# Moving the values' 5x5 depthwise convolution into the attention stage of a four-layer network kernel

## The reference, cut to what matters

```python
x = x + dwconv(x, pos_w, pos_b)                  # 3x3
xn = layer_norm(x, ln1_g, ln1_b)
q, k, v = xn @ q_w + q_b, (xn @ k_w + k_b) * HD ** -0.5, xn @ v_w + v_b
lepe = dwconv(v, lepe_w, lepe_b)                 # 5x5, each channel by itself, 'SAME' edges
q, k = theta_shift(q, sin, cos), theta_shift(k, sin, cos)
o = softmax(q @ k.T + mask) @ v                  # per image and head, 1024 x 1024 scores
x = x + (o + lepe) @ out_w + out_b
```

## Time and profile before

| | |
|---|---|
| three executions | 3669.94, 3670.02, 3678.01 us, median 3670.02 |
| the profiled execution | 3670.32 us |
| its span in the profile | 3668.7 us |
| outside the span | 1.6 us |
| values made token by token | to 219.95 us |
| `depthwise` of the values | 220.2 to 297.3 us |
| attention | 297.9 to 1046.7 us |
| GRU and the later layers | from about 1300 us |
| busy over the whole span | PE 86%, DVE 70%, ACT 50%, POOL 16% |

### The profile page before, as it was taken

The page is one execution under the profiler, slowest core; times in us unless marked ns, Lnnn a source line. Parts: engine busy times, 40 slices in busy tenths (PEclk is TensorE's granted clock), DMA queues, the critical chain, the costliest instruction groups (busy, mean ns, idle before and its releaser), DMA issues. The chain is left out here.

```text
span 3668.7 us, 136690 instructions
## 1 busy us (share of the span) xinstructions
PE 3141.9 (86%) x50394; PEld 2339.4 (64%) x50394; DVE 2582.0 (70%) x12076; ACT 1821.7 (50%) x5594; POOL 583.8 (16%) x2420
## 2 busy tenths in 40 slices
PE   5378999999958947999999999999999998577787
PEld 1134666566622315888988888889888887254454
DVE  4567999999974635777777777777777778466562
ACT  2215999999933025444544444444444445133342
POOL 0001111111100001222222222222222222111110
PEclk9678999999978966555555555555555555678888
DMA  1312333333330000000000000000000000000000
GB/s 32 108 47 95 108 107 107 107 107 107 108 91 1 10 7 2 5 5 5 5 5 5 5 5 5 5 5 5 5 5 5 5 5 4 11 1 1 0 5 13
DMA packets 54608, 116.12 MB, mean 32 GB/s; under 512 B 12313, under 2 KB 19801, under 8 KB 53692
## 3 DMA queue, kind: packets, MB, share of 16 engines
q1 hardware_dynamic: 37104, 53.42, 5.3%
q0 software_dynamic: 13824, 50.34, 3.9%
q10 hardware_dynamic: 2956, 3.15, 0.4%
HBM read 84.06 MB, written 22.81 MB: 29 GB/s over the span
## 5 line engine op out<-in xcount | busy, mean ns | idle before, releaser
L504 PE MATMUL g_zr<-g_hp,g_wp 97*128 97x4 f16 x24576 | 1082.6, 171 | 53.4 <-issue 49.0
L504 PEld LDWEIGHTS g_zr<-g_hp,g_wp 97*128 97x128 f16 x24576 | 956.4, 108 | 157.4 <-issue 51.3
L595 ACT ACTIVATE g_e<-g_tn 96x8 f32<-96x8 f32 x2048 | 437.0, 213 | 557.8 <-DVE g_tn L540 557.8
L480 PE MATMUL g_zr<-s_inner,g_wi 96*128 (+2 forms) x6240 | 585.1, 234 | 61.9 <-issue 39.7
L612 POOL COPY s_y<-g_hs 96x8 f32 x2048 | 401.0, 196 | 1374.9 <-DVE g_hs L555 1374.9
L553 DVE TENSOR_TENSOR_SCAN g_hp<-g_gates,g_e 96x16 f16<-96x16 f32 x2048 | 382.1, 187 | 316.7 <-ACT g_e L595 207.6
L592 ACT ACTIVATE g_gates<-g_zr 96x16 f32<-96x16 f32 x2048 | 399.5, 195 | 315.5 <-PE g_zr L504 315.4
L511 PE MATMUL g_n<-g_hp,g_wp 97*128 97x8 f16 x8192 | 520.1, 174 | 0.0
L844 DVE CUSTOM_DVE_ANT_0 a_negated<-a_scores,a_mask 128x1024 f32<-128x1024 f32 x384 | 468.0, 1219 | 59.1 <-PE a_scores L762 41.2
L870 ACT ACTIVATE a_probs<-a_negated,a_negmax 128x1024 f32<-128x1024 f32 x384 | 442.4, 1152 | 26.1 <-DVE a_negmax L844 16.3
L540 DVE TENSOR_TENSOR_SCAN g_tn<-g_gates,g_n 96x24 f32<-96x24 f32 x2048 | 387.8, 189 | 95.7 <-ACT g_gates L592 95.7
(11 more groups left out here) (324 smaller groups left out, 3058.5 us busy)
## 6 DMA issues: line engine op xcount, KB each, us to landing
a_mask<-in_L_mask POOLq DMA_DIRECT2D x96, 512.0 KB, 5.6
a_k<-k_rows SPq DMA_DIRECT2D x96, 144.0 KB
q_rows<-r_q_parts SPq DMA_DIRECT2D x12, 576.0 KB, 7.4
k_rows<-r_k_parts SPq DMA_DIRECT2D x12, 576.0 KB, 7.4
a_q<-q_rows SPq DMA_DIRECT2D x96, 72.0 KB
o_parts<-a_o_sb SPq DMA_DIRECT2D x384, 18.0 KB
o_part<-o_parts SPq DMA_DIRECT2D x32, 192.0 KB
out_x<-x SPq DMA_DIRECT2D x4, 384.0 KB, 3.0
```

Source lines behind the costliest of these rows:

```text
L480: pe.matmul(o, wi[0:K, half, pw, d * NG + g, :], x, start=first, stop=False, skip_group_check=True)
L504: mm = pe.matmul(zr_bank[u, k][:, 1 - g, d, :, at], wp[0:97, part, (2 * u + d) * NG + g, :], hp[u][0:97, d * NB:(d + 1) * NB, e], start=False,
L595: act.activation(e1[u][:, :, 0], tn[u][:, :, 2], ACT.Tanh, scale=to_tanh).then_inc(n_and_zh[u], 1)
```

## The change

The taps of `lepe` are dealt out anew. `depthwise` is no longer called for the values. At the end of the block that makes `vt`, ACT writes the centre tap of each of the four images into `lepe`, with the bias. The other 24 taps are done in the attention by POOL: 24 taps x 4 images = 96 = the number of groups, so each group does one tap of one image, n = 2 h + half naming the tap and b the image. A tap is two POOL instructions on [96, 1024]: `tensor_scalar` writes window times tap to a new tensor `term`, and `tensor_tensor` adds `term` to `lepe`. A new semaphore `convolved` counts both; POOL waits on it before the add, and before the copy of the next group. POOL's part of the loop over heads is written out for all 12 heads. `lepe_w` and `vpad` are allocated for the whole retention block. `depthwise` gets a parameter `batch` whose default leaves its other calls as they were.

```diff
-def attention(nc, mask, q_rows, k_rows, v_tokens, o_parts):
+BESIDE = (0, 1, 2, 3)
+OTHER_TAPS = [tap for tap in range(25) if tap != 12]
+def attention(nc, mask, q_rows, k_rows, v_tokens, o_parts, vpad, lepe, lepe_w):
...
+        term = sb("term", [C, HH, HH])
+        convolved = sem("convolved")
...
                         po.sem_inc(v_may, 1)
+                        po.wait_ge(convolved, done(g))
                         po.tensor_copy(vs[b % 2][:, :, 0:8], head).then_inc(v_ok, 1)
                         if b == 1 and not (half == 0 and first) and not (last and half == 1):
                             mask_load(h if half == 0 else h + 1, 1 - half, True)
-            heads(po, body)
+                        if b in BESIDE:
+                            convolve(2 * h + half, b, g)
+
+            def done(g):
+                return 2 * sum(i % NB in BESIDE for i in range(g))
+
+            def convolve(n, b, g):
+                tap = OTHER_TAPS[n]
+                dy, dx = tap // 5, tap % 5
+                image = lepe[:, cols(b)].rearrange("c (y x) -> c y x", y=HH)
+                po.wait_ge(v_ok, g + 1)
+                po.tensor_scalar(term[:, :, :], vpad[:, b, dy:dy + HH, dx:dx + HH], lepe_w[:, tap:tap + 1], None,
+                                 ALU.mult).then_inc(convolved, 1)
+                po.wait_ge(convolved, done(g) + 1)
+                po.tensor_tensor(image, image, term[:, :, :], ALU.add).then_inc(convolved, 1)
+
+            for h in range(NH):
+                body(h, h == 0, h == NH - 1)
...
                         act.activation(vt[:, i // 2, (i % 2) * 4:(i % 2) * 4 + 4, :], tokens[i % 2][:, :, 0:C],
                                        ACT.Copy).then_inc(taken, 1)
+                    for b in BESIDE:
+                        act.activation(lepe[:, cols(b)].rearrange("c (y x) -> c y x", y=HH),
+                                       vpad[:, b, 2:2 + HH, 2:2 + HH], ACT.Identity, bias=v["L0_lepe_b"][:, :],
+                                       scale=lepe_w[:, 12:13])
-                depthwise(nc, "r_lepe", [(vpad, lepe_w[:, :], v["L0_lepe_b"][:, :], None, lepe)], 5, 3)
```

More of the change, by code:

```diff
@@ L208, in project, with depthwise @@
             block.vector(take)
-def depthwise(nc, tag, jobs, size, on_tensor):
-    work = [(k, b, half) for k in range(len(jobs)) for b in range(NB) for half in range(2)]
+def depthwise(nc, tag, jobs, size, on_tensor, batch=tuple(range(NB))):
+    work = [(k, b, half) for k in range(len(jobs)) for b in batch for half in range(2)]
     own, shared = work[:len(work) - on_tensor], work[len(work) - on_tensor:]
@@ new lines, in retention_block, with add_bias, _ @@
+            clear(nc, "r_vpad", border(vpad, 2))
+            def add_bias(act, m, b, psum):
+                return act.activation(vpad[:, b, 2:2 + HH, 2:2 + HH], psum.rearrange("p (y x) -> p y x", y=HH),
+                                      ACT.Identity, bias=v["L0_v_b"][:, :])
+            project(nc, "r_v", [xn[0:C, :]], lambda s, m: weights["v_w"][:, :], 1, C, add_bias, "scalar")
+            with ExitStack() as c2:
+                tokens = [c2.enter_context(nc.psum_tensor(f"r_tokens{i}", [128, 4, 128], F)) for i in range(2)]
+                made, taken = c2.enter_context(semaphore(nc, "r_vt_made")), c2.enter_context(
+                    semaphore(nc, "r_vt_taken"))
+                block = c2.enter_context(nc.Block())
+                @block.tensor
+                def _(pe):
+                    for i in range(N // BANK):
+                        if i >= 2:
+                            pe.wait_ge(taken, i - 1)
+                        for k in range(4):
+                            t = i * BANK + k * 128
+                            mm = pe.matmul(tokens[i % 2][:, k, 0:C], xn[:, t:t + 128], vw[:, :], start=True,
+                                           stop=True)
+                        mm.then_inc(made, 1)
+                @block.scalar
+                def _(act):
+                    for i in range(N // BANK):
+                        act.wait_ge(made, i + 1)
+                        act.activation(vt[:, i // 2, (i % 2) * 4:(i % 2) * 4 + 4, :], tokens[i % 2][:, :, 0:C],
+                                       ACT.Copy).then_inc(taken, 1)
+                    for b in BESIDE:
+                        act.activation(lepe[:, cols(b)].rearrange("c (y x) -> c y x", y=HH),
+                                       vpad[:, b, 2:2 + HH, 2:2 + HH], ACT.Identity, bias=v["L0_lepe_b"][:, :],
+                                       scale=lepe_w[:, 12:13])
@@ L1131, in _ @@
                     sp.wait_ge(sent, 16 * sends)
-        attention(nc, d["L0_mask"], q_rows, k_rows, vt, o_parts)
+        attention(nc, d["L0_mask"], q_rows, k_rows, vt, o_parts, vpad, lepe, lepe_w)
         recycle(nc)
```

6 lines of the change are left out of this document (4 added, 2 removed).

## The result

The changed kernel takes 3585.9 us (median of 4 runs, 3584.11 to 3587.7) against 3669.98 for the kernel before on the same chip (4 runs, 3667.72 to 3678.01): a ratio of 0.9767, 95% interval 0.975 to 0.9784. The profiled execution took 3586.61 us, its span is 3584.6 (before 3670.32 and 3668.7).

A forecast was written before the change was run, and what follows sets the result against it. The convolution stage was taken to lie wholly on the path, the attention to be bound by DVE and PE together. Removing 77.34 us and adding 3.90 gives -73.4 us, so 3597 us, range 3588 to 3620.

The forecast's parts named there:

- The stage comes off the path whole: Values' convolution between token block and attention: its removal saves its whole length, 77.34 us.
- The fills: Four ACT centre-tap instructions behind the token copies, on the path: add 3.90 us, upper bound 4.50.
- The row writes: SP's wait on `sent`, formerly behind the convolution: met 20 us before ACT finishes the fills, cost 0.
- the mask DMAs: In the attention, behind POOL's copy: issued at the same time as before, with 22 us to land, cost 0.
- the queue behind the convolution: POOL's next `vs` copy in the attention, waiting for `convolved`: 3.7 us or more to spare, cost 0.
- POOL's taps: 192 POOL instructions in the attention: add 2.363 us, multiply 1.0, about 3.6 a tap, hidden in POOL's waiting.
- DVE beside POOL: In the attention, DVE's two instructions and POOL's taps do not slow each other: 0 us.
- The lock: Rival: in the attention DVE's L844 and POOL's SBUF reads exclude each other, +161 us, 3758; 8 in 100.
- the toll: Rival: each POOL instruction costs DVE 0.1 to 0.3 us in the attention, 3616 to 3655; 7 in 100.
- the yielding: Rival: POOL yields to L844 and bounds the attention, 3693, or 3660 without a gap; 3 in 100.
- The attention at 734 within 5: Sign that the forecast is right: the attention's window stays 734 us within 5.
- the loop written out is more code for POOL only: POOL's written-out loop over heads in the attention: the extra code falls on an engine that waits anyway, cost 0.

The follow-up runs named there:

- e4: Changed kernel with POOL's multiply done twice a tap: 3734.46 us.
- e1: Changed kernel without POOL's 96 taps, POOL's part of the heads a loop again: 3581.4 us.
- e7: Changed kernel with the convolution a stage of its own again, DVE doing three images and POOL the fourth at once, no taps in the attention: 3748.86 us.
- e9: Changed kernel unaltered, run again on another chip: 3577.92 us, median of five runs.
- e12: Changed kernel with 25 tiny matmuls added to PE's program behind the attention: 3555.9 us.
- e10: Changed kernel with 75 tiny matmuls on PE and 75 tiny memsets on DVE added behind the attention: 3608.95 us.
- e8: Changed kernel with centre taps and the clearing of k, q and v on DVE, POOL issuing the first masks at once: 3569.41 us.

## Why the prediction was wrong by 11 us, point by point

- **The stage comes off the path whole**: right. 77.34 us went.
- **The fills**: mis-sized. 4.69 us, neither the 3.90 of the four copies at the start nor the 4.50 of the upper bound. The rows chosen were ACT copies; this is an activation with a factor and a bias for each channel. That is 0.8 us; the attention's opening, 1.0 us shorter, cancelled it.
- **The row writes, the mask DMAs, the queue behind the convolution**: cost 0, right. (The reason for the queue was not: a copy was said to have 3.7 us or more to spare, but by the prediction's own 6.6 us a group with masks leaves 0.9 of 7.49, and in the trace the copy behind it has no wait at all. The distance of six chunks covered it.) DVE's first instruction of the attention moved 73.3 us (238.90 from 312.2) against the 73.4 of the sum.
- **POOL's taps**: add 2378 ns, right (2363). Multiply 2861, taken as 1.0 and bounded at 2.363: wrong, outside both bounds. The upper bound assumed that one input cannot cost more than two. It was hidden, so it cost no time, but the cover was thinner than said: POOL is busy 500 us more, not 320, and 1.2 us a group is left (e4).
- **DVE beside POOL, 0**: right, and shown: e1 (732.5 against 732.3), and e7 for a case in which it is not 0. The lock, the toll and the yielding are out for this kernel. (The yielding rival's lower end, 3660, does not follow from its figures: without a gap between the two, 4.88 + 3.36 us a group is 0.75 us over 7.49, which gives 3669.)
- **The attention at 734 within 5**: right, 732.3.
- **The step that failed**: the sum stopped at the attention. It took all that the diff leaves alone as unchanged, and named "the loop written out is more code for POOL only" as the one effect of code. The 75 matmuls and 75 DVE instructions taken out moved the code of the GRU loop on both engines, and that loop waits for its code 15 times. It gave 15.5 us in the profiled run: 11.1 in PE's stops and 4.4 beside them, less than the 8.4 of DVE's stops that went as well. In e9 it gave 19.9: 11.7 and 8.2. The layers behind it took 5.5 back in the first run and 0.4 in e9, so how far the forecast was off, 11 us, is partly luck: beside its own runs of the kernel before (median 3671.54), e9 is 93.6 us faster, 20 more than forecast. The range's low end, 3588, had 3 us for anything of this kind. The view that would have shown it is the waits of the kernel before, in the longest stage: 88.7 us of "issue" on PE, 15 times at each of two lines, as often as the loop returns. How much it could be is what the padded kernels show: against e9 from 22 us less (e12) to 31 more (e10). Its sign for a given diff can't be read from the profile.

## What to carry to other kernels

Work moved to an engine that waits inside a stage bound by others is free while its mean time per group stays under the stage's, even if single groups overrun (e1, e4). Before moving work to POOL, look at where DVE's inputs lie: beside the two instructions that take a tensor from PSUM it cost nothing, beside those that take all from SBUF both engines lost (e7). Take POOL's price for an operation from that operation in that form: a copy's price says nothing of a multiply's. In a kernel with a long loop, look at the "issue" waits at its returns before any other fine work: a few idle instructions ahead of it moved this one by 22 us, and any edit ahead of it carries an uncertainty of that size.

## What the runs showed of the hardware that was not expected

- POOL multiplies 96x1024 f32 by a factor in 2.86 us, slower than it adds two such tensors (2.38), and copies one in 1.06. The one `tensor_scalar` with multiply and bias on POOL took 1.71 us (e7), less than the multiply alone, and that beside DVE. It ran once, and no run shows why, or whether all taps would be cheaper in that form. DVE does multiply and bias of the same size in 0.81 (e8). The Trainium skill, page "GPSIMD Engine Reference", section "Engine selection", calls operations with one input on POOL roughly line-rate, and those with two about twice as slow as on DVE; the copy's 1.06 fits it, and the multiply's 2.86, above the two-input add's 2.38, speaks against it.
- DVE and POOL both lose when DVE takes two tensors from SBUF: DVE 1.0 us more an instruction, POOL 0.82 and 0.31 (e7). Neither wins.
- A loop's cost at its returns depends on the code ahead of it, and not in the order of its amount: 54 to 89 us in 15 returns, for the same loop.
